# Folding symmetric rows on GpSimd ahead of two cosine and sine transforms, on one core

## The reference, cut to what matters

```python
k = softmax(k, axis=-1)
context = einsum('bhdn,bhen->bhde', k, v)
x_fft = fftn(x, axes=(-2, -1)).real
x_mid = gelu(conv1x1(x_fft, w_q1))
qf = ifftn(conv1x1(x_mid, w_q2), axes=(-2, -1)).real
attnf = softmax(l2norm(qf) @ l2norm(kf).T * temperature)
return conv1x1(attnf @ vf, w_projf)
```

## Time and profile before

| | us |
|---|---|
| median of 3 runs | 3964.45 |
| lowest and highest | 3962.36, 3966.53 |
| the profiled execution | 3964.9 |
| its span | 3963.1 |
| PE busy | 3760.3 (95%) |
| PEld busy | 3091.5 (78%) |
| DVE busy | 3030.4 (76%) |
| ACT busy | 1624.7 (41%) |
| POOL busy | 210.3 (5%) |

### The profile page before, as it was taken

How to read it: one execution, slowest core, us unless ns; L and a number is a source line. 1 busy time by engine, 2 the same in 40 slices (tenths; PEclk the granted TensorE clock), 3 DMA queues, 4 the chain that set the end, 5 groups by cost and what they waited for, 6 DMA issues and landing times.

```text
span 3963.1 us, 56863 instructions
## 1 busy us (share of the span) xinstructions
PE 3760.3 (95%) x21394; PEld 3091.5 (78%) x21394; DVE 3030.4 (76%) x2829; ACT 1624.7 (41%) x2912; POOL 210.3 (5%) x376
## 2 busy tenths in 40 slices
PE   4659999999999999999999999999999999999998
PEld 2348788978799687977889787996879777897977
DVE  7988988789778898679887897789986797753020
ACT  3413662237521564126622375215641266202430
POOL 1001000100001000000001000010001000010000
PEclk8879999999999999999999999999999999999999
DMA  4354222923156221732228231562217322260002
GB/s 112 97 147 112 65 64 44 218 63 77 37 124 168 59 65 39 178 98 65 64 47 214 63 77 40 122 166 60 68 36 194 82 74 55 53 163 25 1 7 30
DMA packets 164717, 344.13 MB, mean 87 GB/s; under 512 B 110336, under 2 KB 110576, under 8 KB 164432
## 3 DMA queue, kind: packets, MB, share of 16 engines
q1 hardware_dynamic: 141392, 255.36, 26.1%
q0 software_dynamic: 23040, 84.95, 9.8%
HBM read 189.27 MB, written 150.99 MB: 86 GB/s over the span
## 4 chain that ended last, share of the span: by engine, by line
PE 77%; DVE 12%; issue 7%; ACT 2%; DMA 1%; POOL 0%; SPq 0%; DVEq 0%; ACTq 0%; POOLq 0%
PE banks L941 15%; PE banks L942 15%; PE banks L947 15%; DVE feat L702 7%; PE banks L979 6%; PE banks L956 6%; PE banks L1009 6%; PE banks L966 4%; PE banks L1021 3%; PE banks L972 2%; PE banks L973 2%; DVE e_lo L725 2%; DMA feat<-feats_d 1%; DVE e_hi L718 1%; PE banks L995 0%
## 5 line engine op out<-in xcount | busy, mean ns | idle before, releaser
L702 DVE SCALAR_TENSOR_TENSOR feat<-xin,w,feat 96x1536 f32<-96x1536 f32 x540 | 943.2, 1808 | 1.1
L941 PE MATMUL banks<-e_hi,wp_hi 96*96 96x384 f32 x1728 | 587.6, 341 | 23.4 <-DVE e_lo L828 12.0
L941 PE MATMUL banks<-e_hi,a_hi 96*96 96x384 f32 x1728 | 591.9, 343 | 15.2 <-ACT a_hi L572 15.2
L942 PE MATMUL banks<-e_lo,a_hi 96*96 96x384 f32 x1728 | 590.1, 342 | 0.0
L942 PE MATMUL banks<-e_lo,wp_hi 96*96 96x384 f32 x1728 | 586.6, 340 | 0.0
L702 DVE SCALAR_TENSOR_TENSOR feat<-xin,wh,feat 96x1536 f32<-96x1536 f32 x288 | 520.5, 1807 | 43.8 <-ACT feat L488 42.9
L702 DVE SCALAR_TENSOR_TENSOR feat<-xin,wv,feat 96x1536 f32<-96x1536 f32 x288 | 520.5, 1807 | 8.9 <-ACT feat L488 8.9
L500 ACT ACTIVATE sqjunk<-feat 96x1536 bf16<-96x1536 f32 x192 | 284.4, 1481 | 258.7 <-DVE feat L702 255.8
L563 ACT ACTIVATE res<-banks 96x768 f32<-96x768 f32 x96 | 77.5, 808 | 689.2 <-PE banks L947 689.2
L947 PE MATMUL banks<-e_hi,a_lo 96*96 96x384 f32 (+1 forms) x1728 | 337.1, 339 | 0.0
L947 PE MATMUL banks<-e_hi,wp_lo 96*96 96x384 f32 (+1 forms) x1728 | 336.1, 338 | 0.0
(11 more groups left out here) (147 smaller groups left out, 4921.7 us busy)
## 6 DMA issues: line engine op xcount, KB each, us to landing
feats_d<-feat SPq DMA_DIRECT2D x160, 576.0 KB, 4.1
feat<-feats_d SPq DMA_DIRECT2D x160, 576.0 KB, 6.5
feat<-in_x SPq DMA_DIRECT2D x48, 576.0 KB, 7.1
res<-in_x POOLq DMA_DIRECT2D x96, 288.0 KB, 4.1
out<-x POOLq DMA_DIRECT2D x96, 288.0 KB, 2.8
out<-res POOLq DMA_DIRECT2D x96, 288.0 KB, 4.4
xin<-in_x SPq DMA_DIRECT2D x32, 792.0 KB, 8.9
xin<-in_x SPq DMA_DIRECT2D x16, 684.0 KB, 9.9
```

The lines of the kernel that those rows point to most:

```text
L702: dve.scalar_tensor_tensor(out=dst, in0=src, scalar=taps_w[d](k), in1=dst, op0=ALU.mult, op1=ALU.add).then_inc(tap_done, 1)
L941: pe.matmul(dst, whi[:, t, :], rows(e_hi, a0, n, dx), start=(t == CENTRE_FIRST[0]), stop=False)
L942: pe.matmul(dst, whi[:, t, :], rows(e_lo, a0, n, dx), start=False, stop=False)
```

## The change

The sums and differences of rows h and 96-h carry all that a cosine or a sine transform along h needs: 49 even rows and 47 odd rows in place of 96 rows. In the kernel after, GpSimd makes them. For the first transform it folds the rows of x ahead of w_q1 (`fold_x`, 13 instructions an image, the large ones of 768 elements a partition). For the second it folds rows of exp(k) (`fold_k`, 47 instructions, most of 192 elements a partition), which ScalarE now writes to a ring of six steps that lies in the tile etile; k and v are taken in the order h, 96-h. Stage 1 becomes two products a channel, 64 columns of weights (49 used rows and 15 more) into PSUM partitions 0 to 63 and 47 columns into partitions 64 to 110, each with 49 moving columns, eight channels in a slot. Stage 2 becomes one product with 111 rows. s1 is a ring of eight. TensorE waits for all of `fold_x` ahead of the row products and for all of `fold_k` ahead of the second transform; ScalarE's exp waits for the fold of the step six before. Unit 8 moves behind `attention_weights`, ScalarE's units go to every 22 slots, and the small products of the first block's attention go to groups 9 and 10 of the convolution.

```diff
-U_DFT = C // 4 + C // 8
+U_DFT = 2 * (C // 8)
+DFT_ORDER = ([(1, g) for g in range(8)] + [(2, g) for g in range(4)]
+             + [(1, g) for g in range(8, 12)] + [(2, g) for g in range(4, 12)])
+X_FOLDS = [(41, 7)] + [(h, 8) for h in range(33, 0, -8)]
-LEAD = 8
+LEAD = 7
-UNIT_USES, UNIT_AT = 20, AT_ROWS + 8
+UNIT_USES, UNIT_AT = 22, AT_ROWS + 8
-HID_AT = 7
+HID_AT = 9
...
+            def fold_x(i):
+                v = x1[0:C, :].rearrange("p (h x) -> p h x", x=W)
+                for h, n in X_FOLDS:
+                    up, down = v[:, h:h + n, :], v[:, H - h:H - h - n:-1, :]
+                    pool.wait_ge(xn_ready, i * XN + -(-(H - h + 1) * W // (N // XN)))
+                    pool.tensor_tensor(xf[:, h:h + n, :], up, down, ALU.add).then_inc(x_folded, 1)
+                    pool.tensor_tensor(xf[:, NV - 1 + h:NV - 1 + h + n, :], up, down, ALU.subtract).then_inc(x_folded, 1)
+                pool.tensor_copy(xf[:, 0:NV:NV - 1, :], v[:, 0:NV:NV - 1, :]).then_inc(x_folded, 1)
...
+                row_evicted(1)
+                fold(1, 1)
+                pool.tensor_copy(z[:, :, 0:NV:NV - 1].rearrange("p c h -> p h c"), krow[:, 0, :, :]).then_inc(k_folded, 1)
+                for g in range(2, U_KV, 2):
+                    row_evicted(g + 1)
+                    fold(g, 2)
...
             def step(b, first, second, more):
                 if second:
                     i = b - 1
+                    fold_x(i)
+                    fold_k(i)
                     pool.wait_ge(gram_done, i + 1)
...
-                    act.activation(z[:, :, 2 * g:2 * g + 2], ps[:, :, 0:C].rearrange("p r c -> p c r"), ACT.Exp)
+                    if g >= KROWS:
+                        act.wait_ge(k_folded, i * K_FOLD_OPS + k_folds((g - KROWS) // 2 + 1))
+                    act.activation(krow[:, g % KROWS], ps[:, :, 0:C], ACT.Exp)
...
-                        for c in range(4):
-                            last = pe.matmul(ps[0:H, c * W:(c + 1) * W], z[:, 4 * g + c, :], w_dft, start=(c == 0), stop=(c == 3),
-                                             skip_group_check=True)
+                        for c in range(8):
+                            cols = slice(c * NV, (c + 1) * NV)
+                            pe.matmul(ps[0:ODD_AT, cols], z[:, 8 * g + c, 0:ODD_AT], w_cos[:, 0:NV], start=(c == 0),
+                                      stop=(c == 7), skip_group_check=True)
+                            last = pe.matmul(ps[ODD_AT:FOLDED, cols], z[:, 8 * g + c, NV:W], w_sin[:, 0:NV],
+                                             start=(c == 0), stop=(c == 7), skip_group_check=True)
...
-                        pe.matmul(d, dcos, s1[:, g % 2, :, 0:NV], start=True, stop=False)
-                        last = pe.matmul(d[:, :, 1:NV - 1], dnsin, s1[:, g % 2, :, NV:W], start=False, stop=True)
+                        last = pe.matmul(ps[0:H, 0:8 * NV], dh[:], s1(g).rearrange("p c v -> p (c v)"), start=True, stop=True)
...
                 maxes(i)
+                pe.wait_ge(x_folded, (i + 1) * X_FOLD_OPS)
...
+                pe.wait_ge(k_folded, (i + 1) * K_FOLD_OPS)
                 dft(i, AT_DFT2)
```

More of the change, by code:

```diff
@@ L60, with k_folds @@
 USES = AT_E + U_E
[L63 to L68, removed]
-assert len(DFT_ORDER) == U_DFT
+DFT_ORDER = ([(1, g) for g in range(8)] + [(2, g) for g in range(4)]
+             + [(1, g) for g in range(8, 12)] + [(2, g) for g in range(4, 12)])
+assert len(DFT_ORDER) == U_DFT
+NO = W - NV
+ODD_AT = 64
+FOLDED = ODD_AT + NO
+S1 = 8
+KROWS = 6
+X_FOLDS = [(41, 7)] + [(h, 8) for h in range(33, 0, -8)]
+X_FOLD_OPS = 2 * len(X_FOLDS) + 1
+def k_folds(n):
+    return 2 * n + 1 if n else 0
+K_FOLD_OPS = k_folds(H // 4)
 CENTRE_FIRST = (4, 0, 1, 2, 3, 5, 6, 7, 8)
@@ L252, in rows, with s1 @@
             return buf[:, at:at + n * EP].rearrange("p (r c) -> p r c", c=EP)[:, :, 0:W]
+        def s1(g):
+            return s1a[:, g % S1] if g % S1 < 3 else s1b[:, g % S1 - 3]
         def small_chain(eng, s, total, i):
@@ L310, in _ @@
             loads = [(mats[:, n, :], a[k]) for n, k in enumerate(
-                ("ident", "group", "mask", "negmask", "w_dft", "dcos", "dnsin", "wq", "wq1", "wq2", "wq2t", "wpft"))]
+                ("ident", "group", "mask", "negmask", "w_cos", "w_sin", "wq", "wq1", "wq2", "wq2t", "wpft"))]
+            loads += [(dh[:], a["dh"])]
             loads += [(wkv[0:C, :], a["wkv"]), (wh[:], a["wh"]), (wv[:], a["wv"]), (w45[:], a["w45"]),
@@ L855, in step @@
                 if first:
-                    for u in range(2, LEAD):
+                    for u in range(2, LEAD + 1):
                         taps(b, u)
-                    dve.wait_ge(tap_done, unit_taps(b, LEAD - 1, KT - 1, 0 if first_image(b) else 1))
+                    last_use = UNITS - 5
+                    assert last_use == LEAD
+                    dve.wait_ge(tap_done, unit_taps(b, last_use, KT - 1, 0 if first_image(b) else 1))
                     if first_image(b):
-                        dve.wait_ge(last_dir_sums, LEAD)
+                        dve.wait_ge(last_dir_sums, last_use + 1)
                     edge_rows(b, NCH - 1)
-                    taps(b, LEAD, 0, LEAD_TAPS)
                 if second:
@@ L866, in step @@
                 if first:
-                    taps(b, LEAD, LEAD_TAPS)
                     for u in range(LEAD + 1, UNITS):
@@ L978, in ctx_rows @@
                 for r in range(2):
-                    last = pe.matmul(ctx_ps[0:C, 0:C], vrow[:, g % VROWS, r, :], z[:, :, 2 * g + r],
+                    last = pe.matmul(ctx_ps[0:C, 0:C], vrow[:, g % VROWS, r, :], krow[:, g % KROWS, r, :],
                                      start=(g == 0 and r == 0), stop=(g == U_KV - 1 and r == 1))
@@ L993, in attention_block @@
                     for r in range(TR):
-                        h = g * TR + r
-                        last = pe.matmul(ps[0:W, r * C:(r + 1) * C], x1[0:C, h * W:(h + 1) * W], wq1,
+                        last = pe.matmul(ps[0:W, r * C:(r + 1) * C], xf[:, g * TR + r, :], wq1,
                                          start=(r == 0), stop=(r == TR - 1), skip_group_check=True)
@@ L1007, in attention_block @@
                         for r in range(2):
-                            h = 2 * g + r
+                            h = (g, H - g)[r] if g else (0, H // 2)[r]
                             last = pe.matmul(ps[0:W, r * 2 * C:(r + 1) * 2 * C], x1[:, h * W:(h + 1) * W], wkv[:],
```

54 lines of the change are left out of this document (36 added, 18 removed).

## The result

The changed kernel takes 4172.57 us (median of 4 runs, 4166.87 to 4179.79) where the kernel before takes 3965.49: 1.0524 times as long, interval 1.0506 to 1.0543, slower. The forecast was 3984 with a range up to 4120; the time lies above the range, inside what the second rival gave (4062 to 4181). The profiled execution took 4166.87 us, its span is 4165.3.

The account below looks back on a forecast made before the run. TensorE, 77% of the chain, was taken as the bound. Seven mixed steps at +3.9 us (13.5 lost, 9.6 gained) give +27.3, the last image -7.6: 3964.9 + 19.7 = 3984.6 profiled, so 3984 us, range 3870 to 4120.

Parts of the forecast that it names:

- the second rival: GpSimd folds and VectorE taps take turns, lengthening a mixed step by 15 to 32 us: 4062 to 4181, chance 0.29.
- I take the first end: Stage 1: loads and matmuls of both column tiles stand in one line, 1.65 us for eight channels, 4.1 less a transform.
- the first rival: Stage 1's column tiles run side by side, 0.91 us for eight channels, 13.0 less a transform: 3887 us, chance 0.30.
- The stage 2 of the forecast: Transforms: the sine product's 0.63 us goes and the cosine product's 0.66 stays.
- 2.55 that TensorE takes for two steps: Steps of k and v: TensorE's time for two steps, 2.55 us, against which the folds of exp(k) were priced.
- The folds of x: GpSimd beside the maxima: 7.9 to 23.7 us an image within 24.7 available, so they cost nothing.
- That the folds do not slow VectorE is a choice: Steps of k and v: VectorE's taps assumed undisturbed by GpSimd's folds of exp(k), at no cost.
- That GpSimd keeps up: Steps of k and v: folds of exp(k) take 0.16 to 0.49 us each, and the ring of six steps covers the delay.
- the last fold: Ahead of the second transform: only the last pair of exp(k) folds shows, 0 to 1.2 us, taken as 0.6.
- The first transform's waits: ScalarE's pieces add some 4 us to the first transform; with fewer slot copies half comes back, range 0 to 4.
- Behind the convolution's start: VectorE's moved unit delays attention's third sum, which the new image's convolution awaits: 9.9 to 17.1 us lost, taken as 13.5.
- The sum: Whole kernel: a mixed step +3.9 us, seven times +27.3, and the last image -7.6, giving 3984 us.

Follow-up runs that it names:

- e11: The kernel before with the 13 GpSimd folds of x added beside the maxima, their results read by nobody: 4087.76 us, 1.0302 of the kernel before.
- e1: The changed kernel with every GpSimd fold replaced by two memsets that read nothing and last at least as long: 3918.85 us, 0.9881 of the kernel before.
- e7: The changed kernel with each fold replaced by one memset of the same rows, and unit 8 put back ahead of the attention weights: 3840.03 us.
- e8: The changed kernel with real folds and only the moved unit put back ahead of the attention weights: 4218.42 us, 1.0632 of the kernel before.
- e5: The changed kernel with each GpSimd fold replaced by one memset of the same rows: 3803.81 us, 0.9590 of the kernel before.
- e4: The changed kernel with real folds and the four VectorE taps between the maxima moved ahead of them: 4123.87 us, 1.0405 of the kernel before.
- e10: The changed kernel with each GpSimd fold of x held until a certain maximum has been taken: 4100.16 us, 1.0331 of the kernel before.
- e2: The changed kernel with only the folds of x replaced by memsets of at least their length: 4040.74 us, 1.0191 of the kernel before.

## Why the prediction was wrong

**Stage 1: wrong, and for the faster.** The step that failed is "I take the first end", the column tiles in one line at 1.65 for eight channels. The timeline of one stage 1 in the last image, and then the chain behind it (start us, us, engine, line, count):

```profile
3906.11 0.26 PE L1026 MATMUL banks<-mats,z 96*64 96x49 f32 x1
...
3906.20 0.22 PE L1026 MATMUL banks<-mats,z 96*64 96x49 f32 x1
3906.24 0.21 PE L1028 MATMUL banks<-mats,z 96*47 96x49 f32 x1
3906.26 0.22 PE L1026 MATMUL banks<-mats,z 96*64 96x49 f32 x1
```

```profile
3913.77 2.80 PE banks L1032 x8
3920.44 5.44 PE banks L1032 x16
3925.88 1.95 PE banks L1068 x12
```

The even tile (L1026) and the odd one (L1028) start 0.02 to 0.04 apart and overlap. Eight groups of eight channels take (3913.77 - 3906.11) / 8 = 0.96, where the forecast had 1.65 and the first rival 0.91; a transform is 19.6 in place of 27.7, and 18.8 by the rival. The Trainium skill, TensorEngine Tiling (Array Packing), Tiling Modes, has different tiles load and multiply in parallel; the trace agrees, by these 0.96. The stage 2 of the forecast, 0.66, is right: 2.80 / 4 = 0.70 and 5.44 / 8 = 0.68.

**k and v: a term that wasn't there.** The step "2.55 that TensorE takes for two steps" was carried over from the strided read, though the change moves the context products to the ring. It is 1.98, and 14.7 an image less, more than either transform gave. Four context matmuls take 0.66 with their elements 384 bytes apart and 0.34 side by side (3625.98 to 3626.32). The Trainium skill, SBUF — State Buffer, section Door 1: The DMA port swizzle, says that consecutive accesses within one line of 16 bytes run at full rate and that each new line costs; these two numbers agree with its direction.

**The folds of x: right that they end in time, wrong that this makes them free.** In the last image they take 21.4 us in 13 instructions, inside the 7.9 to 23.7, and end 2.5 ahead of the rows; in the mixed steps 22.7 to 24.3, and 17 to 20 ahead, since the maxima last longer. But the step priced them against the row products only, and left the four taps beside them to the second rival, at "about 4". e11 shows that term alone: 18.0 in the median of seven steps, 122 us in the total.

**The folds of exp(k): the decisive step.** "That the folds do not slow VectorE is a choice" was the wrong one, and k and v take 84.2 instead of the 49 that TensorE needs (64.5 before, by the same borders; the prediction's 61 starts later). That GpSimd keeps up was right: alone a fold takes 0.59, more than the 0.49 at most that was forecast. The second rival had the mechanism, and its test, a wait of more than 0.73 a fold on average, is passed: the first folds of a pair (L436) take 1.82 on the mean where one alone takes 0.59. That the time falls into its 4062 to 4181 is in part luck, for its sizes were wrong in two ways that partly cancelled: it knew the alternation (2.28 a tap and fold, by its terms; 2.07 measured) but not the stop that lasts as long as the other engine's queue, and it didn't have the gain of the ring. That a whole queue passes, not one instruction, is what 16.96 and 20.78 showed. The Trainium skill, SBUF — State Buffer, Who interferes with whom, excepts a GpSimd instruction that only writes, and e1 agrees (the mean tap is 1806 ns); that the one which starts first keeps the ports for its own whole length is too little for this case, where a queue of nine folds and a copy kept them. A further loss was in neither: the clock. After 7.4 us of waiting for the last fold, the second transform starts at 0.50 and has 0.67 to 0.70 on the mean, 27.9 instead of 20.4.

**The first transform's waits and the last fold.** What ScalarE's pieces add to the first transform was read as some 4 us and is 1.6 (33.4 in the mixed steps, 31.8 in the last image). After the change 0.4 of it is left (20.0 against 19.6), so 1.2 came back where 2 was forecast. The last fold was to show by 0.6; alone it is 0.49 (the last image), beside taps 7.4.

**Behind the convolution's start: right in mechanism and size.** A loss of 13.5 was forecast, 9.9 to 17.1; it is 15.2, and e7 and e8 show it gone with the unit put back (240.1 and 239.2). TensorE's wait for the x sums, forecast as 10 to 17, is 11.9. That the convolution of the old image starts earlier by what the transforms gain failed with the steps ahead of it.

**The sum.** Forecast +3.9 a step. Measured by the same steps: first transform -13.4 (33.4 to 20.0), k and v -15.4 and second transform -12.2 (to the last image's 49.1 and 20.4), then folds and taps +17.9 and +35.1, the second transform at the low clock +7.5, behind it +15.2: +34.7, against 34.9 from the starts of the maxima. With the tiles and the ring forecast right and nobody shut out, the time would have been near that of e5, 3804; that is an estimate, since e5's writes are shorter than folds. So the chances went wrong in both ways at once: the first rival's tiles and the second rival's turns came true together, a case that the prediction gave 0.02, and that as a way to become faster.

## What to carry to other kernels

A second engine's work is not hidden because it ends before its reader: ask first what it reads, and which instructions of a neighbour it can shut out for as long as its queue is full. A stretch in which the neighbour is idle (here the last image, without taps) shows what each would take alone. And when one edit holds several changes, price each alone: here the place that the context products read from was worth 109 us (3967.47 to 3858.08), and the rest, with the folds where they are, cost 314 more (4172.57 against 3858.08).

## What the runs showed of the hardware

- A GpSimd instruction with two SBUF inputs and a VectorE instruction with two can stop each other for as long as the one has further instructions queued without a gap: 16.96 us for a tap of 1.8, 20.78 for a fold that takes 0.39 alone. At other places they alternate, a fold 2.11 and a tap every 2.07. Every fold that stood out a whole queue (after, e4, e8, e10, seven each) met a run of 24 to 28 taps without a gap; every fold there and in e2 that met the first or second tap of a run got through in 3.14 or less. A tap that met the third or fourth fold of x in a run took 16.8 to 18.5, one that met the first 2.5 to 2.7 (after). That does not hold for every kind of fold: in e8, taps that met the 8th to 29th fold of exp(k) in a row took 2.28 at most. No edit tried the length of the run, so what decides is open.
- GpSimd memsets into SBUF leave taps alone (mean 1806 ns); GpSimd copies wait for taps (20.65) but delay them by 0.5 at most (longest tap 2.30).
- A moving operand with its elements 384 bytes apart made a 96 x 96 fp32 matmul take 0.165 us instead of 0.085 (four in 0.66 and 0.34).
- Two column tiles of 64 and 47 columns run beside each other in fp32: 0.96 us for 32 matmuls of 49 columns, loads included.
- In e5 stops of 2.35 to 3.97 us on TensorE, with no releaser in the profile, came early in four second transforms with a mean clock of 0.76 to 0.82; in the one with a stop of 2.09 it stayed at 1.00. What stopped TensorE is open.
